# The row's peak as the bias of ACT's exponential in six layers of local attention, in place of a subtraction on DVE

## What is computed

```python
for i in range(6):
    x = attn_layer(shift_tokens(x), Wqkv[i], q_scale[i], k_scale[i], Wo[i]) + x
    x = ffn_layer(shift_tokens(x), ln_g[i], ln_b[i], W1[i], b1[i], W2[i], b2[i]) + x

def attn_layer(x, Wqkv, qs, ksc, Wo):
    q, k, v = split_heads(x @ Wqkv)
    q = rotary(l2norm(q) * qs, scale)
    k = rotary(l2norm(k) * ksc, 1 / scale)
    sim = einsum(q, k) * 8.0                  # QK_SCALE
    sim = where(outside_window, -big, sim)
    return softmax(sim) @ v, heads merged, @ Wo
```

## Time and profile before

| | |
|---|---|
| median of 3 runs | 2713.26 us (2708.19 to 2714.23) |
| span of the profiled execution | 2713.2 us |
| PE busy, matmuls | 2525.8 us, 93% |
| DVE busy | 2253.2 us, 83% |
| POOL busy | 1737.4 us, 64% |
| ACT busy | 1560.3 us, 58% |
| granted clock of PE, by fortieths of the span | 8 or 9 tenths in the first eight, 9 or more after |

### The profile page before, as it was taken

How to read it: one execution, slowest core, us unless ns; L and a number is a source line. 1 busy time by engine, 2 the same in 40 slices (tenths; PEclk the granted TensorE clock), 3 DMA queues, 4 the chain that set the end, 5 groups by cost and what they waited for, 6 DMA issues and landing times.

```text
span 2713.2 us, 62249 instructions
## 1 busy us (share of the span) xinstructions
PE 2525.8 (93%) x18693; PEld 2059.1 (76%) x18693; DVE 2253.2 (83%) x5097; ACT 1560.3 (58%) x3463; POOL 1737.4 (64%) x1485
## 2 busy tenths in 40 slices
PE   6999799989999899999999998999989999899998
PEld 4774577768887688886788867888768888688886
DVE  4778788878998699996899978999778989699995
ACT  3545455656665466664666655666546666466663
POOL 3444311168886487884788747887657888388883
PEclk9998899989999999999999999999999999999999
DMA  3000000100000100000000001000010000000000
GB/s 86 0 0 0 1 0 0 40 25 0 0 0 4 38 1 0 0 0 17 25 0 0 0 8 34 0 0 0 8 33 0 0 0 0 17 1 0 0 0 16
DMA packets 27720, 24.09 MB, mean 9 GB/s; under 512 B 11734, under 2 KB 24164, under 8 KB 26852
## 3 DMA queue, kind: packets, MB, share of 16 engines
q1 hardware_dynamic: 27620, 22.96, 2.9%
HBM read 21.90 MB, written 1.05 MB: 8 GB/s over the span
## 4 chain that ended last, share of the span: by engine, by line
PE 57%; DVE 17%; issue 8%; ACT 4%; DVEq 1%; POOL 1%; ACTq 0%; POOLq 0%
PE bank L688 10%; PE bank L728 7%; PE bank L754 6%; PE bank L715 5%; PE bank L493 5%; DVE l_ss L1434 4%; DVE xs_part L1411 4%; PE bank L701 4%; DVE l_rot L1424 4%; ACT l_sq L1032 3%; PE bank L742 3%; PE bank L693 3%; PE bank L645 2%; PE bank L710 2%; PE bank L634 1%
## 5 line engine op out<-in xcount | busy, mean ns | idle before, releaser
L443 POOL TENSOR_TENSOR l_rn<-l_ss,minus_half 128x8 f32<-128x8 f32 x384 | 632.3, 1647 | 192.6 <-DVE l_ss L1444 171.7
L441 POOL TENSOR_TENSOR l_qk<-l_rot 128x512 f32<-128x512 f32 x384 | 488.1, 1271 | 164.5 <-DVE l_rot L1424 162.0
L447 POOL TENSOR_TENSOR l_qk<-l_qk,l_rn 128x512 f32<-128x512 f32 x384 | 400.5, 1043 | 55.0
L1037 ACT ACTIVATE l_qkT<-bank 128x512 f32<-128x512 f32 x384 | 229.4, 597 | 334.2 <-PE bank L701 334.1
L1032 ACT ACTIVATE l_sq<-bank 128x512 f32<-128x512 f32 x384 | 229.9, 599 | 312.1 <-PE bank L688 302.5
L728 PE MATMUL bank<-l_v,probT 128*128 128x65 f32 x3072 | 389.4, 270 | 9.0 <-ACT probT L893 8.9
L728 PEld LDWEIGHTS bank<-l_v,probT 128*128 128x128 f32 x3072 | 374.8, 192 | 13.3 <-ACT probT L893 12.6
L1420 DVE TENSOR_TENSOR l_rot<-bank,l_tab 128x512 f32<-128x512 f32 x384 | 264.1, 688 | 139.6 <-ACT l_sq L1032 139.4
L1132 DVE TENSOR_REDUCE peak<-bank 128x4 f32<-128x512 f32 (+1 forms) x512 | 348.3, 680 | 36.8 <-PE bank L531 30.3
L688 PE MATMUL bank<-w_high,xs_part 128*128 128x512 f32 x768 | 341.7, 445 | 33.8 <-DVE xs_part L1411 33.8
L888 ACT ACTIVATE prob<-sm 128x512 f32<-128x512 f32 x512 | 319.1, 623 | 83.5 <-DVE sm L1140 77.3
(11 more groups left out here) (187 smaller groups left out, 4761.7 us busy)
## 6 DMA issues: line engine op xcount, KB each, us to landing
early<-in_L_ffn_Wqkv_dram SPq DMA_DIRECT2D x6, 1536.0 KB, 6.6
l_wo<-in_L_ffn_Wo_dram SPq DMA_DIRECT2D x6, 512.0 KB, 3.6
f_w<-in_L_ffn_W_dram SPq DMA_DIRECT2D x6, 341.0 KB
out_dram<-X SPq DMA_DIRECT2D x4, 256.0 KB, 2.3
f_w<-in_L_ffn_W_dram SPq DMA_DIRECT2D x6, 128.0 KB
l_oT<-in_L_xattn_Wkv_dram SPq DMA_DIRECT2D x1, 512.0 KB, 5.7
const<-in_const_dram SPq DMA_DIRECT2D x1, 392.0 KB, 3.1
f_b<-in_L_ffn_b_dram SPq DMA_DIRECT2D x24, 0.5 KB
```

Of the source, the lines that this page charges most:

```text
L441: pool.tensor_tensor(l_qk[:, k], l_rot[:, k, 0], l_rot[:, k, 1], ALU.add).then_inc(l["add_done"], 1)
L443: pool.tensor_tensor(l_rn[:, k], l_ss[:, k], minus_half[:], ALU.pow).then_inc(l["rn_done"], 1)
L447: pool.tensor_tensor(v, v, l_rn[:, k, :, None].broadcast_to([128, 8, L_DIM]), ALU.mult).then_inc(l["qk_done"], 1)
```

## The change

ACT reads the scores of the local layers from banks 3 and 4, with one instruction for each head, 128 columns each, whose bias is that head's peak with its sign turned. DVE's `l_shift` is gone from its list, and the peaks are taken with `negate`. The scale 8 no longer stands in the exponential but is multiplied once into the q half of the table `l_sc` on POOL, before the tables are made. Both PE waits for `sub_done` in the local layers are now waits for `exp_done`. The two cross attentions keep the subtraction and the old `exp`.

```diff
+            pool.tensor_scalar(l_sc[:, :, 0], l_sc[:, :, 0], QK_SCALE, None, ALU.mult).then_inc(scaled_q, 1)
+            pool.wait_ge(scaled_q, 1)
...
                 def l_scores(u, b, j):
                     pe.wait_ge(l["qkT_done"], upto(ub, u + 1))
-                    pe.wait_ge(l["sub_done"], upto(ub, u))
+                    pe.wait_ge(l["exp_done"], upto(ub, u))
...
                     if i == 0:
-                        pe.wait_ge(l["sub_done"], upto(ub, UNITS))
+                        pe.wait_ge(l["exp_done"], upto(ub, UNITS))
...
+                def l_exp(u, b, j):
+
+                    k = j % 2
+                    act.wait_ge(l["peaked"], upto(ub, u + 1))
+                    act.wait_ge(l["turned"], upto(ub, u - 1))
+                    for r in range(2):
+                        for p in range(2):
+                            n = 2 * r + p
+                            ins = act.activation(prob[:, k, n * 128:(n + 1) * 128],
+                                                 bank[:, 3 + r, p * 128:(p + 1) * 128], ACT.Exp,
+                                                 bias=peak[:, k, n:n + 1])
+                    ins.then_inc(l["exp_done"], 1)
...
-                                      (5, lambda u, b, j: exp(l, ub, u, j, QK_SCALE)), (7, l_copy_o), (3, l_copy_qk),
+                                      (5, l_exp), (7, l_copy_o), (3, l_copy_qk),
...
                 def l_peaks(u, b, j):
-                    find_peaks(l, ub, u, j, bank[:, 3:5, 0:256].rearrange("p a (b n) -> p a b n", b=2), 4)
+                    dve.wait_ge(l["s_done"], upto(ub, u + 1))
+                    dve.wait_ge(l["exp_done"], upto(ub, u - 1))
+                    dve.tensor_reduce(peak[:, j % 2, 0:4], bank[:, 3:5, 0:256].rearrange("p a (b n) -> p a b n", b=2),
+                                      AX.X, ALU.max, negate=True).then_inc(l["peaked"], 1)
...
-                def l_shift(u, b, j):
-                    subtract_peaks(l, ub, u, j, bank[:, 3:5, 0:256].rearrange("p a (b n) -> p a b n", b=2))
...
-                return Pipeline(dve, [(0, l_copy_in), (1, l_split_x), (4, l_peaks), (2, l_floor), (4, l_shift), (6, l_divide),
+                return Pipeline(dve, [(0, l_copy_in), (1, l_split_x), (4, l_peaks), (2, l_floor), (6, l_divide),
```

More of the change, by code:

```diff
@@ L231, in build @@
         preset = sem("preset")
-        tables = sem("tables")
+        tables, scaled_q = sem("tables"), sem("scaled_q")
         passed = {nc.vector.engine: sem("passed_dve"), nc.gpsimd.engine: sem("passed_pool")}
```

## The result

The changed kernel takes 4083.07 us (median of 4 runs, 4060.76 to 4087.86) against 2713.74 for the kernel before in the same comparison: a ratio of 1.503, with a 95% interval of 1.498 to 1.507. The forecast was 3553 with a range of 3290 to 3710. The direction, the place of the stop and its length came out as forecast; the time lies far above the range.

The account below looks back on a forecast made before the run. PE's own issue was taken to set the pace, at work 93% of the span. 2713.2 us plus 724 for the new waits, 1 for POOL's scaling and 115 for the clock gave 3553 us, range 3290 to 3710.

Parts of the forecast that it names:

- The new wait and its place: Local layers: PE stops once per slot before mask and scores, until ACT's four exponentials, queued behind probT, are done.
- Its length: PE's stop: four exponentials take 1.18 us; mask later by 2.04 us in A and B, 2.25 in C, 2.94 in D.
- A: Slot (one PE pass through its stages) of a four-slot local-layer batch, with the output projection; 5.80 us before the change.
- B: The plain slot of a local-layer batch; 4.00 us before the change.
- C: The slot of a local-layer batch with the turning of x; 4.80 us before the change.
- D: The slot of a local-layer batch with ACT's copies of x; 4.93 us before the change.
- The sum of the waits at the full clock: Local layers: 7.79 us per batch over 96 batches, 748 us, less 24 at layer starts and ends: 724 us.
- The waits of C and D: PE's waits for DVE's xin and split and ACT's copies of x vanish behind the stop: 1.48 us back per batch.
- DVE's relief worth nothing: Local layers: dropping DVE's subtraction saves 264 us of its busy time but nothing on the path.
- The clock: PE's idling in the stop brings one low-clock stretch per batch: 115 us, bounds 0 and 230.
- The clock goes in every slot: Rival: each PE stop brings its own clock fall, costing 460 us, total about 3900 us; chance 0.12.
- The rivals of a gain and of a covered stop: Gain: score banks free in time, 2594 us, chance 0.02. Covered: half of 724 us returns, about 3100 us, chance 0.03.

Follow-up runs that it names:

- 15 products: The changed kernel with 15 idle 128x256 matmuls issued by PE in each local-layer slot before the wait for the exponentials: 3396.39 us, ratio 1.251.
- the reordered versions: The changed kernel with ACT's exponential moved ahead in its list, or PE's scores moved later: from 3175.53 us down to 2813.00 us for the best.
- Stops of 1.3 us in all four slots: The changed kernel with ACT's exponential put ahead of probT and of the copies of x: 3175.53 us, ratio 1.170.
- 1.3 us in three and 2.1 in the fourth: The kernel before with only PE's scores' wait moved from the subtraction to the exponential, subtraction and single exponential kept: 3428.92 us, ratio 1.263.
- 7 products: The changed kernel with 7 idle 128x256 matmuls issued by PE in each local-layer slot before the wait for the exponentials: 3573.82 us, one run.

## Why the prediction was wrong

**The new wait and its place: right.** PE stops once in each slot, between the transposition and the mask, with the exponential as releaser (786 of the mask's 790 us of idle time).

**Its length: right.** Mask 1.97 us later in A, B and C (2.04 forecast for A and B, 2.25 for C, where 0.21 had been added for a late start that the middle slot does not have), and 2.8 in D (2.94 forecast), read in the run with 15 products, where the clock does not blur it: 3.26 against 0.44 before. The four exponentials take 1.14 us against 1.18.

**The sum of the waits at the full clock: right within 6%.** 724 us forecast, 3396 - 2713 = 683 measured, or up to some 710 with what the products shorten. The waits of C and D in front of xin, xsT and xs_part went as forecast: 1.8, 0 and 5.2 us are left of 25.5, 26.2 and 33.8.

**DVE's relief worth nothing: right here.** The waits that it could have shortened are gone. In the reordered versions no gain from it is seen either, but no run takes it apart from the later exponentials.

**The clock: wrong, and this is the step that failed.** "I take one low stretch for each batch, of about 3.4 us, as short as a fall seen here can be, with PE at work some 70% of it: 1.2 us lost, 115 us over 96 batches." Its upper bound was 230. Measured: 655 to 687 us, about 7 us for each batch. The number and the length of the low stretches were both too small. The record of the granted clock holds 273 stretches at the low level, 2.8 for each batch, of 5.8 us on average. In the steady loop one begins in every one of 84 slots D, in 78 of 84 slots A, in 59 of 84 C and in 28 of 102 B. In the trace before, a single stop of 1.9 us without a fall had been taken as a sign that A, B and C would mostly be spared. That held for B alone. That a stop which comes back every 6 us weighs more than a single one fits this, but why A and C fall so much more often than B, with the same stop of 1.81 us, stays open. The price of a low stretch was nearer: with 15 products the low level was granted for about 75 us, so some 1515 us more of it cost 655 to 687 us, 0.43 to 0.45 us for each, against 1.2 / 3.4 = 0.35 assumed.

**The rivals.** "The clock goes in every slot", with a chance of 0.12, came nearer than the forecast: falls begin in nearly every slot A and D and in most C, but not in most B. Its 460 us were too few all the same, since a fall cost about 2.5 us (687 / 273) and not 1.2. The rivals of a gain and of a covered stop are refuted: the banks are never free in time while the exponential stands behind probT, and 683 of the 724 us are lost at the full clock.

**Short stops and the clock.** Where the Trainium skill (TensorE: Matmul & The Clock Gate, A second HAM failure mode: psum-queue depth-cycling) describes a PE that idles briefly between groups of matmuls and whose clock swings between its levels, this kernel's trace agrees: stops of 1.8 us, and of 2.8 in D, in slots of 6 to 11 us, and 273 low stretches where the kernel before has 11.

## What to carry to other kernels

Before moving work between engines, write down for the waiting engine what stands in the other's queue ahead of the thing it will wait for. Here one changed wait turned a release that came a slot early into one that could not come before PE's own latest product had been copied, and cost 471 us at the full clock. And a stop of PE that recurs is to be priced twice, as its length and as the clock that it takes down: idle products of 256 columns, which here left the slots' lengths at the full clock as they were to within 0.1 us, measure the second part nearly alone.

## What was unexpected in the hardware

The number of falls for a stop of a given length. Stops of 1.3 us in all four slots gave a clock of 0.970, with 37 low stretches; 1.3 us in three and 2.1 in the fourth, 0.919, with 103; 1.0 in three and 1.9 in the fourth (7 products), 0.934, with 86, of which 71 begin in the fourth; 1.81 in three and about 2.8 in the fourth, 0.805, with 273. The one longer stop in four slots matters most in this series, but the runs don't vary it alone. In the last case the low level was granted for 39% of the span, and slots A, with the long output projection, took 11.0 us for 7.8 of work and waiting at the full clock.

Four activations of 128 columns with a bias operand took 1.14 us, that is 0.26 us from one to the next and 0.37 for the last. The Trainium skill (ScalarE: Activation LUTs, What ACT_TABLE_LOAD costs) gives figures from which 1.26 us was estimated. The measurement is 0.12 us shorter: these instructions overlap by about 0.12 us, where the page has 0.09, which makes 0.07 us over three overlaps, and one takes 373 ns where the page's figures come to 386, which makes the other 0.05.
